# Attention and its feed-forward on eight cores: order of the start, sharing of two engines' work at both ends, and all eight banks for the last block

## The reference, cut to what matters

```python
h = layernorm(x)                       # eps 1e-5, no weights
lam = 2 / (1 - |h|^2)
# q and k: hyperbolic layers with weights z and bias b
inner = h @ (z / |z|)
v = 2 |z| * arcsinh(lam * inner * cosh(2b) - (lam - 1) * sinh(2b))
w = sinh(v);  q_or_k = w / (1 + sqrt(1 + |w|^2))
V = h @ w_v.T + b_v
a = softmax(q k^T / 8) V               # per head
x = x + layernorm(a)
h = layernorm(x);  hp = h shifted by one token
r = sigmoid((mu_r h + (1-mu_r) hp) @ W_r.T)
k = relu((mu_k h + (1-mu_k) hp) @ W_k.T) ** 2
x = x + layernorm(r * (k @ W_v.T))
```

## Time and profile before

| | |
|---|---|
| median of 3 runs | 1936.33 us (1933.95 to 1937.82) |
| the profiled execution | 1944.02 us, span of its slowest core 0: 1942.5 us |
| spans of the cores | 1907.3 to 1942.5 us, mean granted clock 0.941 to 0.954 |
| PE busy | 1617.3 us (83%) |
| ACT busy | 1371.1 us (71%) |
| DVE busy | 1127.6 us (58%) |
| POOL busy | 138.8 us (7%) |
| DMA | 210 MB, mean 108 GB/s |

### The profile page before, as it was taken

How to read it: one execution, slowest core, us unless ns; L and a number is a source line. 1 busy time by engine, 2 the same in 40 slices (tenths; PEclk the granted TensorE clock), 3 DMA queues, 4 the chain that set the end, 5 groups by cost and what they waited for, 6 DMA issues and landing times.

```text
span 1942.5 us, 20758 instructions; the slowest of 8 cores (1907.3 to 1942.5 us)
## 1 busy us (share of the span) xinstructions
PE 1617.3 (83%) x7286; PEld 542.3 (28%) x7432; DVE 1127.6 (58%) x1917; ACT 1371.1 (71%) x1322; POOL 138.8 (7%) x181
## 2 busy tenths in 40 slices
PE   0556665899988998968899999998999999999845
PEld 0222222233332333212233323322322323333322
DVE  2668956796655555544751473374374275285984
ACT  0034644899988897999888878887877888885000
POOL 1101100111010000000000010010000000010000
PEclk9978887999998999989999999999999999999978
DMA  9578673565362437934541262353254244162321
GB/s 162 111 65 94 48 78 103 145 173 106 77 110 63 91 85 96 165 110 151 170 127 57 77 195 77 95 173 83 83 164 100 84 165 128 57 192 56 103 65 44
DMA packets 175970, 210.00 MB, mean 108 GB/s; under 512 B 120064, under 2 KB 128768, under 8 KB 175872
## 3 DMA queue, kind: packets, MB, share of 16 engines
q1 hardware_dynamic: 155120, 145.29, 31.0%
q0 software_dynamic: 20752, 63.38, 16.9%
HBM read 143.80 MB, written 50.46 MB: 100 GB/s over the span
## 4 chain that ended last, share of the span: by engine, by line
PE 56%; DMA 16%; DVE 14%; ACT 8%; issue 3%; SPq 1%; POOL 1%; DVEq 0%; POOLq 0%
PE p_fil L451 22%; PE psc L760 12%; PE p_att L787 11%; PE p_att L791 9%; ACT pt L776 4%; DMA xa<-x 2%; DMA xn_fm<-xn_tm 2%; DMA qsl<-s_q 2%; DMA c_att<-s_att 2%; DMA c_xf<-c_xtm 2%; DMA s_v<-v_st 1%; DVE w L490 1%; PE psc L451 1%; DMA out<-c_x 1%; DMA attn_tm<-af 1%
## 5 line engine op out<-in xcount | busy, mean ns | idle before, releaser
L776 ACT ACTIVATE pt<-psc 128x1024 bf16<-128x1024 f32 x1024 | 1031.6, 1034 | 208.2 <-PE psc L764 194.1
L760 PE MATMUL psc<-qsl,ksl 64*128 64x512 bf16 x1024 | 402.3, 393 | 71.5 <-ACT pt L776 32.0
L764 PE MATMUL psc<-qsl,ksl 64*128 64x512 bf16 x1024 | 403.3, 394 | 0.0
L787 PE MATMUL p_att<-pt,vsl 128*128 128x512 bf16 x963 | 381.0, 396 | 23.5 <-DVE af L841 14.7
L791 PE MATMUL p_att<-pt,vsl 128*128 128x512 bf16 x1007 | 390.2, 387 | 9.4 <-issue 5.4
L760 PEld LDWEIGHTS psc<-qsl,ksl 64*128 64x128 bf16 x1024 | 95.0, 93 | 512.8 <-issue 512.8
L451 PE MATMUL p_fil<-xn_fm,w 128*128 128x512 bf16 x769 | 199.3, 389 | 11.3 <-DVE w L490 6.5
L451 PE MATMUL p_fil<-c_xk,w 128*128 128x512 bf16 x501 | 147.5, 388 | 34.7 <-DVE c_xk L1019 25.1
L841 DVE CAST af<-p_att 65x512 bf16<-65x512 f32 x128 | 81.9, 679 | 152.2 <-PE p_att L791 152.0
L787 PEld LDWEIGHTS p_att<-pt,vsl 128*128 128x128 bf16 x1024 | 99.0, 97 | 246.3 <-issue 226.3
L451 PE MATMUL p_fil<-w,c_ka 128*128 128x512 bf16 x505 | 144.7, 387 | 6.0 <-DVE c_g L1074 5.4
(11 more groups left out here) (133 smaller groups left out, 1697.1 us busy)
## 6 DMA issues: line engine op xcount, KB each, us to landing
vsl<-s_v SPq DMA_DIRECT2D x64, 520.0 KB, 5.1
ksl<-s_k SPq DMA_DIRECT2D x63, 512.0 KB, 4.2
xa<-x SPq DMA_DIRECT2D x32, 512.0 KB, 5.5
c_x<-x SPq DMA_DIRECT2D x32, 512.0 KB, 7.5
out<-c_x POOLq DMA_DIRECT2D x32, 512.0 KB, 4.7
s_v<-v_st POOLq DMA_DIRECT2D x32, 260.0 KB, 13.9
s_k<-w POOLq DMA_DIRECT2D x8, 1024.0 KB, 8.4
s_q<-w POOLq DMA_DIRECT2D x8, 1024.0 KB, 7.4
```

The costliest lines, as they stand in the source:

```text
L760: T(lambda t: t.matmul(reg[:, 0:512], ksl[sl][0:64, c * 128:(c + 1) * 128], qsl[sl][0:64, :], start=True, stop=True, skip_group_check=True ...
L764: tok = T(lambda t: t.matmul(reg[:, 512:1024], ksl[sl][64:128, c * 128:(c + 1) * 128], qsl[sl][64:128, :], start=True, stop=True, skip_gro ...
L776: B["exp"][g] = S(lambda s: s.activation(pt[g % NPT][:], psc[g % 2][:], AF.Exp, scale=0.125), [B["q"][g], B["pvg"].get(g - NPT)], 1.03)
L787: T(lambda t: t.matmul(p_att[0][:, :], vsl[sl][:, c * 130:c * 130 + 128], po[:, 0:512], start=(c == 0), stop=(c == 15), skip_group_check=T ...
```

## The change

**Start.** Three x tiles are loaded first; the three weights come one after the other: `zk` waits for the third tile, the others are put into POOL's queue when the one before is estimated to be there. The order of sequence 0 is k0, k1, v0, v1, k2, q0, k3, v2, v3. The squares of the weights are made in pieces of 1024 columns in buffers of `pt`. The bias of the values is added by one more matmul per group in sequence 0 (`extra`), so that the eviction is a copy. Attention starts when k0, k1, k2 and q0 are done and k3 is projected (before: four tails done, all values projected, k3 projected). The first pair's keys and values are loaded block by block (`first_pair`), and `ready` now asks for the last value block too.

**Sharing.** `on_act` compares the estimated backlog of ScalarE and VectorE; before attention and after it, it sends to ScalarE the second operation of `ball_evict`, the value evictions, the scaling before the last exps (as the scale of eight exps of 512 columns), `c_xtm`, the relu of `k_evict` and one addition of `c_last`.

**Pacing.** `dve()` holds an operation back until VectorE's estimated backlog is under 0.4 us. Several estimated latencies change; `group` may be 1.6 us ahead (`AHEAD`) when behind its quota.

**Stage C.** Work goes by tile of 128 tokens (`c_tile`, `c_last`), with 12 instead of 8 buffers of `x1`, and three instead of two blocks in flight; the quota is 1200. The last attention block goes from `attn_tm` straight to `C["att"]`. When the last pair is out, all eight banks are used.

```diff
@@ first_weights, load_xa
+    def first_weights():
+        yield p.till(lnA["xtok"][2])
+        for slot, n in enumerate(["zk", "wvT", "zq"]):
+            W[n] = load_w(slot, n, [lnA["xtok"][2] if n == "zk" else None])
+            yield p.till(W[n]) - 1.0
+    def on_act(ds, dv):
+        return alone["act"] and p.busy["s"] + ds < p.busy["v"] + dv
+    def dve(slack=0.4):
+        while p.busy["v"] > p.now + slack:
+            yield p.busy["v"] - p.now - slack
@@ norm_setup
-            t0 = V(lambda v, h=h: v.tensor_mul(
-                w8[2][:], w_sb[slot][:, h * 4 * D:(h + 1) * 4 * D],
-                w_sb[slot][:, h * 4 * D:(h + 1) * 4 * D]), [wz, tok], 2.3)
+            for ci in range(4):
+                wc = w_sb[slot][:, (h * 4 + ci) * D:(h * 4 + ci + 1) * D]
+                t0 = V(lambda v, wc=wc, ci=ci: v.tensor_mul(
+                    pt[ci][:], wc, wc), [wz, tok], 0.62)
@@ group
+        if extra:
+            T(lambda t, bi=bi: t.matmul(
+                banks[bi], extra[0], extra[1], start=True, stop=False,
+                skip_group_check=True),
+                list(waits) + [extra[2], tk_cst, bank_free[bi]])
-            while p.busy["t"] > p.now + (0.9 if late() else 0.25):
-                yield pe_ready(0.9 if late() else 0.25)
+            while p.busy["t"] > p.now + (AHEAD if late() else 0.25):
+                yield pe_ready(AHEAD if late() else 0.25)
@@ ball_evict
+        if on_act(0.63, 0.41):
+            un["tok"][dc] = S(lambda s_: s_.activation(
+                w8[wi][:, dc * QB:(dc + 1) * QB],
+                w8[wi][:, dc * QB:(dc + 1) * QB], AF.Identity,
+                scale=smcol(cq, dc), bias=smcol(sq, dc)), [tu], 0.63)
@@ a_tail_half
+        by_act = on_act(2.5, 1.4)
+        if by_act:
+            for j in range(4):
+                dc = h * 4 + j
+                t7 = S(lambda s_, dc=dc, j=j: s_.activation(
+                    hb[:, j * QB:(j + 1) * QB], wt[:, dc * QB:(dc + 1) * QB],
+                    AF.Exp, scale=smcol(tz, dc)), [t5], 0.63)
+                t8 = S(lambda s_, dc=dc: s_.activation(
+                    wt[:, dc * QB:(dc + 1) * QB],
+                    wt[:, dc * QB:(dc + 1) * QB],
+                    AF.Exp, scale=smcol("m" + tz, dc)), [t7], 0.63)
@@ first_pair, ready, attention
+    def first_pair():
+        for b in range(NQB):
+            while (0, b, "k") not in A["done"]:
+                yield 0.2
+            B["ld"][0][0][b] = dma("y", lambda y, b=b: y.dma_start(
+                out=ksl[0][:, b * QB:(b + 1) * QB],
+                in_=s_k[0][0, :, b * QB:(b + 1) * QB]), "kfirst%d" % b,
+                [A["kst"][(0, b)]])
+            while (0, b) not in A["vblk"]:
+                yield 0.2
+            B["ld"][0][2][b] = dma("y", lambda y, b=b: y.dma_start(
+                out=vsl[0][:, b * 520:(b + 1) * 520],
+                in_=s_v[0][0, :, b * 520:(b + 1) * 520]), "vfirst%d" % b,
+                A["vblk"][(0, b)] + [tk_vpad])
-        return ((s, qb, "q") in A["done"] and (
-            i == 0 or all((s, b, "k") in A["done"] for b in range(NQB))))
+        return ((s, qb, "q") in A["done"] and (s, NQB - 1) in A["vblk"] and
+                all((s, b, "k") in A["done"] for b in range(NQB)))
@@ b_norm
+            to = C["att"][tt] if (s, qb) == LAST else att_st[j]
+            if (s, qb) == LAST:
+                B["att_store"][(s, qb, tt)] = tn
+                continue
@@ c_last
+        while n == len(order_c) - 2 and n + 1 not in C["mixr"]:
+            yield 0.3
@@ c_firsts
-            while n >= 2 and "fin_%d" % (n - 2) not in C:
+            while n >= 3 and "fin_%d" % (n - 3) not in C:
@@ the end of build_nc
+    for tt in range(3):
+        load_xa(0, 0, tt)
+    M.add(first_weights())
-    M.add(a_proj([("k", 0, 0), ("v", 0, 0), ("k", 0, 1), ("v", 0, 1),
-                  ("q", 0, 0), ("k", 0, 2), ("v", 0, 2), ("v", 0, 3),
-                  ("k", 0, 3)], lambda: True, 0.5))
+    M.add(a_proj([("k", 0, 0), ("k", 0, 1), ("v", 0, 0), ("v", 0, 1),
+                  ("k", 0, 2), ("q", 0, 0), ("k", 0, 3), ("v", 0, 2),
+                  ("v", 0, 3)], lambda: True, 0.5))
-    M.run(lambda: len(A["done"]) >= 4 and "k" in A["used"].get((0, 3), ())
-          and A["v_n"] == 16 and not any(bank_busy[2:]))
+    M.run(lambda: (0, 2, "k") in A["done"] and (0, 0, "q") in A["done"]
+          and "k" in A["used"].get((0, 3), ()))
     ring["n"] = 2
+    M.run(lambda: not any(bank_busy[2:]))
+    alone["act"] = False
-    M.add(c_seconds(lambda: B["pairs"] == 64 or fill["n"] < 1344 *
+    M.add(c_seconds(lambda: B["pairs"] == 64 or fill["n"] < 1200 *
                     (B["g"] - g0) / (1023 - g0)))
-    M.run(lambda: B["pairs"] == 64)
+    M.run(lambda: 63 in B["evac"])
+    ring["n"] = 8
+    alone["act"] = True
```

More of the change, by code:

```diff
@@ L221, in load_w @@
             in_=w_in[name].rearrange("(c p) d -> p c d", p=128)),
-            "w%d" % slot, waits, w_at[0] - p.now)
+            "w%d" % slot, waits, 33.0)
     def wchunk(slot, ci, lo, hi):
@@ L274, in norm_setup @@
                           else ("cqq", "sqq", "tzq", "nsq"))
+        while ("zk" if which == "k" else "zq") not in W:
+            yield 0.3
         wz = W["zk" if which == "k" else "zq"]
@@ L438, in a_ln, with group @@
         A["lam"][(s, b)] = tl
-    def group(lhs, rhs, waits, late):
+    def group(lhs, rhs, waits, late, extra=None):
         bi = take_bank()
@@ L551, in a_proj @@
                 yield gap
+            while {"k": "zk", "v": "wvT", "q": "zq"}[which] not in W:
+                yield 0.3
             if which == "v":
@@ L612, in a_tail_half @@
         yield p.till(t5)
-        t6 = None
-        for j in range(4):
+        t6 = t7 = t8 = None
+        by_act = on_act(2.5, 1.4)
+        for j in range(0 if by_act else 4):
             dc = h * 4 + j
+            yield from dve()
             t6 = V(lambda v, dc=dc: v.tensor_scalar(
@@ L802, in attention @@
         emit_loads(0)
+        M.add(first_pair())
+        while 0 not in B["ld"][0][0]:
+            yield 0.2
         emit_qk(0)
@@ new lines, in c_first @@
+        if b == 0:
+            xf = C["xf"][:].rearrange("p (c t) -> p c t", c=NCH)
+            while n >= 1 and n - 1 not in C["mix"]:
+                yield 0.3
+            C["halo"] = V(lambda v: v.memset(xf[:, :, 15:16], 0.0),
+                          [C["xf_free"]], 0.2)
+        for tt in range(4):
+            while (s, b, tt) not in B["att_store"]:
+                yield 0.3
+            while C["att_busy"][tt]:
+                yield 0.3
+            if (s, b) == LAST:
+                ta = B["att_store"][(s, b, tt)]
+            else:
+                ta = dma("y", lambda y, tt=tt: y.dma_start(
+                    out=C["att"][tt][:],
+                    in_=s_att[s][b * QB + tt * 128:
+                                 b * QB + (tt + 1) * 128, :]),
+                    "catt%d" % tt, [B["att_store"][(s, b, tt)],
+                                    C["att_free"][tt]], 3.0)
+            C["att_busy"][tt] = True
+            M.add(c_tile(n, s, b, tt, ta, tx[tt]))
@@ L999, in c_first @@
-        C["c1"][n] = tx
+        j = tt % 2
+        while C["xtm_busy"][j]:
+            yield 0.2
+        C["xtm_busy"][j] = True
+        yield p.till(C["xtm_free"][j])
+        xf = C["xf"][:].rearrange("p (c t) -> p c t", c=NCH)
+        yield from dve()
+        if on_act(1.06, 0.81):
+            t1 = S(lambda s_: s_.activation(
+                C["xtm"][j][:], x1[:], AF.Identity, scale=smt((n, 2, tt)),
+                bias=smt((n, 3, tt))), [n3, C["xtm_free"][j]], 1.06)
+        else:
+            t1 = V(lambda v: v.tensor_scalar(
+                C["xtm"][j][:], x1[:], smt((n, 2, tt)), smt((n, 3, tt)),
+                ALU.mult, ALU.add), [n3, C["xtm_free"][j]], 0.81)
@@ L1067, in gate, with gated @@
         give_bank(bi, got["t"])
-    def gated(bi, tok, tt, j, hf, got, tg, out):
+    def gated(bi, tok, tt, j, hf, got, tg, last):
         yield p.till(tok)
@@ L1082, in gated @@
         if len(tg) == 2:
-            out.append(stats(C["g"][tt], C["st"][8 + tt], C["mv"][2], tt,
-                             tg))
+            M.add(last(tg, tt))
     def c_second(n, s, b, late):
@@ L1102, in c_second @@
         C["xk_used"].append(tok)
[L1103 removed]
+        while n not in C["mixr"]:
             yield 0.2
[L1105 removed]
         for tt in range(4):
```

403 lines of the change are left out of this document (219 added, 184 removed).

## The result

The changed kernel takes 1887.7 us (median of four) where the kernel before takes 1937.1 beside it: ratio 0.9743, interval 0.9722 to 0.9765. The forecast was 1826; the gain is some 50 us of the 110 forecast. The time lies in the range, near the one of rival A. The profiled execution (slowest core, 4) has a span of 1888.2 us, 54.3 under that of before.

What follows compares the result with a forecast made beforehand. The middle was taken as near one engine's limit (ScalarE, then PE), with waits at both ends, VectorE's in the head. Head 75 + middle 5 + end 30 = 110; 1944-110-7.7 = 1826 us, 8-in-10 range 1775 to 1892.

Steps and rivals of the forecast that it cites:

- rival A: Early attention start fails: gate at chunk 2 holds, value blocks come last; head gains only 20 to 34; about 1880; chance 0.22.
- The head: Stretch to 337 us, projections and tails of sequence 0: 75 us to be gained, bounds 34 and 108.
- better pacing: Head: holding each wide operation until VectorE's queue is within 0.4 us takes some 5 us more, 263 to 258.
- the 17.0 of the store burst: Head: value stores beside a transpose delayed projections once; x normalized before most stores removes this, 17 us.
- The work: Head: moving shares of three operation kinds to ScalarE takes 8+9+11 = 28 us off VectorE, leaving 183.
- X first: Head: loading three x tiles before the weights starts the first projection near 54 instead of 71.78, 17 us.
- The share of the queues: Head: x beside weight loads gets a quarter of the bandwidth; with even turns half, and about 12 us less gain.
- What is late next is the value stores: Head: v2 and v3, last on two banks, have stores landing near 215 to 230, just under the fifth tail.
- The middle: From 337 to 1776 us, attention with projections, then feed-forward: 5 us gained, bounds -10 and +25.
- The end: After attention, from 1776 us: last block's wait 17, eight banks 8.5, last tile 6.3; 30 taken, bounds 10 and 42.
- The last tile: End: only one tile's work after the last matmul, 5.8 instead of 12.1 us, saves 6.3.
- Rival C: Middle: filler 1.6 us ahead delays scores, ScalarE waits more than is given back; slower, 1966 at 0.2 us each; chance 0.05.

## Why the prediction was wrong

**The head, 75 us forecast, 0 measured.** The step that failed is "idle 126-17-17-12 = 80, with 183 of work gives 263; better pacing [...] 258". Up to the fourth exp the changed kernel has 113 us of VectorE idle and 239 of work, 352 in all. Each part of the step went wrong in its own way.

The idle time: the waits that were to shrink did, and by more than was counted, for x from 55.3 to 9.2 us, for projections (the 17.0 of the store burst) from 21.5 to 0.9. Others grew in their place, for value stores from 10.1 to 36.4 us, for transposes from none to 19.3. A wait taken away was counted as time gained, without a look at what VectorE would stand at next.

The work: 28 us were to leave VectorE. Of the 56 second operations of `ball_evict` 21 went to ScalarE (9 us, at 0.81 us each there where 0.6 was forecast) and of the 32 value evictions 5 (3 us). Of the multiplications before the last exps none went, all 48 are on VectorE:

```profile
L670 DVE TENSOR_SCALAR w<-w,smc 128x512 bf16<-128x512 bf16 x48 | 14.0, 346 | 0.0
L528 ACT ACTIVATE w<-w,smc 128x512 bf16<-128x512 bf16 x21 | 17.1, 813 | 37.0 <-DVE w L521 36.9
```

And 26 tiles are normalized instead of 18, some 22 us, since the gap before the fifth tail's end left room in which sequence 1 was begun.

The end of k3's tail: it is a chain of its own, which starts when a pair of bh comes free and goes at the written pace. The forecast read neither the order of the tails nor the 4.4 us. Three edits bring it forward, each by itself: the pace of 2.8 us (k3's store at 314 against 338 on that chip), VectorE's queue without its bound (308 against 338), and the order of before, in a run that also changes a wait (295). So the "better pacing" that was to take 5 us more had the wrong sign in the head: the bound costs 24 us of loads there and pays them back in the middle. And none of the three brings the fourth exp near 262 us.

With the pace loosened, a good part of what was forecast for the head comes, though most of it after 350 us. On one chip, without the 32, the changed kernel at pace 2.0 has 1013 loads at 350 us and 3316 at 900; the kernel before at 2.8 has 951 and 3056. That is 13 us and 56 us; in time it is 0.9479 against 0.9944.

**X first, 17 us.** The first projection came at 64.1, not 54. VectorE stood 12.6 us for a transpose between 24 and 37 us, and nine tiles, not seven, were normalized before it. With x first undone, the projection was earlier still and the time 37 us longer. What x first is worth is therefore not the start of the first projection. Shown is where the loads are lost (between 350 and 1100 us at the pace of 4.4, before 900 us at 2.8) and that the granted clock of the head is lower (0.83 against 0.85, and 0.80 against 0.91); since the other arrival also makes another written order, which of the two does it stays open.

**The share of the queues.** zk, now alone on its queue, landed 19.5 us after its issue. In that time its queue moved 2.10 MB in 1040 packets and SyncE's queue, with x and the transposes, 1.00 MB in 1345. So a third of the bytes was left for x, where the forecast counted a quarter and its alternative a half. The rule behind that half (the Trainium skill, DMA: Bandwidth & Descriptors, "Queues, rings and completion order") speaks of turns by packet and not of equal bytes; the forecast took one for the other. Whether the turns were even the trace doesn't show.

**"What is late next is the value stores ... just under the fifth tail"**: the last was issued at 254.6, and the tail came 100 us later. VectorE and ScalarE do wait 53 us for these stores in the head; moving them to another queue left these waits and the time as they were. What the time would be without them no run shows.

**The middle, 5 us forecast, 34 measured**: the mechanism was named, the size was not. The bounds were read from PE's busy time, 837 of 876 us, in which the matmuls missing from the trace look like idle time and a slower clock like work. "The quota was never reached, so the smaller one does not bind hard" left out that the lead can lift the filler: with 1.6 us 1197 of the 1536 are done by attention's end, and without it 1069. Lead and quota were worth 13 to 18 us where they were tried, and the bound on VectorE's queue 18 us of loads in one stretch; the two are the causes shown. The x1 buffers and the work by tile, which the forecast named first, were not tried alone.

**The end, 30 forecast, 20 measured**, and 25 with the same number of matmuls left. "0 to 24 left, I take 8" for the wait before the last block: 20.7. The direct way through SBUF gave nothing measurable; why is not shown. Eight banks: 8.5 forecast; eight instead of four are worth about 3, and against two they were not tried. The last tile: 3.8 of the 6.3.

**Rival A** had the time (1880), by luck: it has 20 to 34 us from the head and 5 from the middle, where the loads show 0 and 34. The gate at a later chunk gained nothing, and of the stores only their queue was tried. **Rival C** did not decide: from 950 to 1772 us ScalarE waits 129.5 us for scores in 309 places, 5 us more than in the earlier trace rows, and the stretch is faster.

## What to carry to other kernels

Follow each chain that releases the next stage (its buffers, its order and any pace written by hand) to its last operation; the sum of the busiest engine's work does not tell when it ends, because freed time is filled with other work and with other waits. Count completed work (weight loads) at fixed times in both traces: it shows in one view where time is won and where it is given back. A pace set by hand for one kernel should be tried again after the kernel changes: here one number was worth as much (2.5 per cent) as the whole change, and in the kernel before it 0.6 per cent. The same holds for a bound that helps in one stage: the one on VectorE's queue gained in the middle and cost in the head. Setting it by stage was not tried.

## What the hardware showed that was not expected

The same program up to attention's end differs between chips by more than many edits. Where the kernel before takes 1937 us, the changed one has 924 and 929 loads at 350 us in two profiles and takes 1886 us; on two other chips it has 977 and 959, and with small edits to its end takes 1866 and 1869 us.

Busy time of PE is no measure of its work in a stretch at a varying clock: in two runs of the first 350 us, 221 us of it held 960 loads at a granted 0.80, and 228 us held 1093 at 0.91.

The 260-KB value stores, of 260-byte runs, go out 7.7 to 8.3 us apart once three buffers are full (230.80, 238.55, 246.25, 254.55). From the other queue the eight of that burst were issued within 37 us instead of 43, and the waits of VectorE and ScalarE for them came to 54 us against 53.
